# Output products with features on the partitions, in three passes of split operands, the first half's one behind Q and K of the next round

## What is computed

```python
xn  = layernorm(x)                                   # (4, 1024, 128)
q, k, v = heads(xn @ Wq), heads(xn @ Wk), heads(xn @ Wv)   # 16 heads of 64
w = softmax(causal(q @ k.T / 64))                    # per head
w = w * mask; w = w / (sum(w) + 1e-8)                # mask: a ramp over the keys
attn = merge_heads(w @ v) @ Wo                       # (4, 1024, 128)
ffn  = dequant(clip(round(xn / scale))) @ (ternary - 1).T + bias
out  = x + attn + ffn
```

## Time and profile before

| | |
|---|---|
| time, median of 3 runs | 1000.46 us (1000.36 to 1007.18) |
| the profiled execution's own time | 1000.45 us |
| its span in the trace | 998.7 us |
| PE busy | 983.3 us, 98% |
| DVE busy | 756.3 us, 76% |
| POOL busy | 706.4 us, 71% |
| ACT busy | 451.4 us, 45% |
| largest groups of the chain that ended last | G 25%, S 23%, M 12%, Y 7%, D 6% |

### The profile page before, as it was taken

The page is one execution under the profiler, slowest core; times in us unless marked ns, Lnnn a source line. Parts: engine busy times, 40 slices in busy tenths (PEclk is TensorE's granted clock), DMA queues, the critical chain, the costliest instruction groups (busy, mean ns, idle before and its releaser), DMA issues.

```text
span 998.7 us, 19217 instructions
## 1 busy us (share of the span) xinstructions
PE 983.3 (98%) x7125; PEld 633.6 (63%) x7125; DVE 756.3 (76%) x1706; ACT 451.4 (45%) x607; POOL 706.4 (71%) x649
## 2 busy tenths in 40 slices
PE   8999999999999999999999999999999999999997
PEld 4565666666666666666666666666666666666654
DVE  7877888878788878787767777777777667777754
ACT  4444445444444444454443454443454444454442
POOL 8766767767767667867766767667767667777672
PEclk9999999999999999999999999999999999999999
DMA  6000000000000000000000000000000000000000
GB/s 177 3 2 2 2 1 3 2 3 2 2 22 3 2 2 2 1 2 2 2 12 13 1 3 2 2 2 3 1 2 23 3 2 2 1 3 2 2 2 22
DMA packets 16133, 8.52 MB, mean 9 GB/s; under 512 B 5404, under 2 KB 15644, under 8 KB 16040
## 3 DMA queue, kind: packets, MB, share of 16 engines
q1 hardware_dynamic: 15416, 7.15, 2.6%
q10 hardware_dynamic: 624, 0.14, 0.1%
HBM read 4.33 MB, written 2.10 MB: 6 GB/s over the span
## 4 chain that ended last, share of the span: by engine, by line
PE 86%; DVE 9%; issue 2%; POOL 1%; ACT 1%; DMA 1%; DVEq 0%; SPq 0%; ACTq 0%; POOLq 0%
PE pv L1025 25%; PE ring L1008 23%; PE ring L970 12%; PE beside L1067 7%; PE beside L1040 6%; DVE ring L770 3%; PE ring L943 3%; PE ring L939 3%; PE ring L940 3%; DVE v L757 3%; DVE beside L794 1%; PE beside L1055 1%; PE beside L977 1%; PE ring L957 1%; PE ring L958 0%
## 5 line engine op out<-in xcount | busy, mean ns | idle before, releaser
L569 ACT ACTIVATE prob<-ring 128x1024 f32<-128x1024 f32 (+3 forms) x384 | 293.6, 810 | 346.7 <-PE ring L1008 346.6
L503 POOL TENSOR_TENSOR psumd<-psumd,prob 128x512 f32<-128x512 f32 (+1 forms) x250 | 406.2, 1625 | 28.9 <-POOL psumd L503 1.3
L770 DVE CUSTOM_DVE_ANT_0 ring<-ring,causal 128x128 f32<-128x128 f32 (+3 forms) x512 | 240.4, 517 | 97.1 <-PE ring L970 96.3
L1008 PE MATMUL ring<-q,k 64*128 64x512 f32 (+3 forms) x2304 | 279.8, 347 | 2.3 <-DMA mrow<-maxrow 0.8
L1025 PE MATMUL pv<-prob,v 128*64 128x512 f32 (+3 forms) x1536 | 267.1, 490 | 0.0
L476 POOL TENSOR_SCALAR_AFFINE_SELECT prob<-prob 128x256 f32<-128x256 f32 x256 | 109.4, 429 | 217.0 <-ACT prob L569 214.9
L1008 PEld LDWEIGHTS ring<-q,k 64*128 64x128 f32 x2304 | 194.6, 185 | 37.6 <-DVE rowmax L770 5.2
L1025 PEld LDWEIGHTS pv<-prob,v 128*64 128x64 f32 x1536 | 104.9, 137 | 154.1 <-issue 142.0
L774 DVE TENSOR_REDUCE rowmax<-ring 128x2 f32<-128x1024 f32 x128 | 151.4, 1222 | 3.9 <-PE ring L970 0.5
L499 POOL TENSOR_TENSOR psumd<-prob 128x768 f32<-128x768 f32 (+1 forms) x63 | 132.5, 2103 | 24.2 <-ACT prob L569 19.1
L970 PE MATMUL ring<-k,q 64*128 64x512 f32 (+3 forms) x768 | 142.9, 408 | 3.0 <-DVE k L746 0.7
(11 more groups left out here) (120 smaller groups left out, 943.3 us busy)
## 6 DMA issues: line engine op xcount, KB each, us to landing
kext<-kext SPq DMA_DIRECT2D x128, 4.0 KB, 1.7
out<-x_sb SPq DMA_DIRECT2D x8, 256.0 KB, 2.4
x_sb<-in_L_attn_query SPq DMA_DIRECT2D x3, 512.0 KB, 5.5
mrow<-maxrow SPq DMA_DIRECT2D x62, 4.0 KB
x_sb<-in_L_attn_query SPq DMA_DIRECT2D x2, 256.0 KB, 4.3
xn_sb<-in_L_attn_Wv SPq DMA_DIRECT2D x1, 512.0 KB, 5.2
wo<-in_L_attn_Wo SPq DMA_DIRECT2D x1, 512.0 KB, 7.0
xn_sb<-in_L_attn_Wq SPq DMA_DIRECT2D x1, 448.0 KB, 3.5
```

What stands on the lines that cost most here:

```text
L503: g.tensor_tensor(acc[:, :, lo:HALF], acc[:, :, lo:HALF], pr[:, :, lo:HALF], ALU.add).then_inc(acc_done, 1)
L569: a.activation(prob[n % NPROB][:, :, lo:HALF], ring[:, slot(f"S{t}", i), :, lo:HALF], ACT.Exp, scale=1.0 / DH).then_inc(exp_done, 1)
L770: last = v.tensor_tensor_reduce(out=ring[:, s, h, 0:n], in0=ring[:, s, h, 0:n], in1=causal[:, HALF - n:HALF], scale=1.0, scalar=MASKED, op ...
L1008: last = t_.matmul(ring[:, s, h, lo:HALF], k[p][rows, keys], q[p][rows, cols], start=(at == 0), stop=(at == len(parts) - 1))
```

## The change

Y of all pairs but the last one is now computed with features on the partitions: the weights `Wo` stand still, and the 512 tokens of a half move through in one matmul. Wo and the values are split as for Q and K, so that three float32r matmuls of 512 columns take the place of four float32 ones of 128. The products of a batch's pairs are summed in `yt` (in the place of xn of batch 0); after the last pair **P0** and **P1** turn the sum back on PE (4 transposes each), and DVE adds it to `x_sb`. The high part of the values (**h0**, **h1**) is a copy on ACT, the rest (**l0**, **l1**) a subtraction on DVE of two operands in SBUF. There is one buffer each for `o_sb`, its high part and its rest. The last pair keeps the old form.

The order changes too. Y0 goes from behind M9 to the next round, behind Q and K. Y1 goes from between M5 and M6 to where Y0 was. The quantisation runs one pair later, norm3 of the last batch moves to rounds 16 and 17, and Wo is loaded early, split on ACT and POOL in round 0 (**wo**). P stands in rounds 9, 17, 25 and 31.

```diff
-PE_PLAN = ("T Q+ K+ X0 X1 W G11- M0+ M1+ S0 S1 S2 M2+ D1- M3+ S3 V+ S4 S5 M4+ S6 M5+ Y1- M6+ M7+ S7 D0 G3 "
-           "M8+ S8 S9 S10 M9+ Y0 M10+ M11+ S11 G7")
-ACT_PLAN = "Z Qhi+ Khi+ X0 X1 E0 E1 E2 ln1- ex1- E3 E4 E5 E6 E7 ln0 ex0 E8 E9 E10 E11"
-DVE_PLAN = ("Tc Z Qlo+ Klo+ R0+ R1+ X0 X1 W R2+ R3+ t1- u1- Vs+ o1- R4+ R5+ Ya1- R6+ R7+ t0 u0 R8+ o0 q "
-            "R9+ R10+ Ya0 R11+")
-POOL_PLAN = "L0 A0 L1 A1 L2 A2 L3 A3 B0 A4 A5 A6 A7 L8 L9 L10 L11 A8 A9 A10 A11 B"
+PE_PLAN = ("T Q+ K+ P0 Y0- G11- P1 X0 X1 W M0+ M1+ S0 S1 S2 M2+ D1- M3+ S3 V+ S4 S5 M4+ S6 M5+ M6+ M7+ S7 D0 G3 "
+           "M8+ S8 S9 S10 M9+ Y1- M10+ M11+ S11 G7")
+ACT_PLAN = "Z Qhi+ Khi+ X0 X1 wo E0 E1 E2 ln1- ex1- E3 E4 E5 E6 h1- E7 ln0 ex0 E8 E9 E10 E11 h0"
+DVE_PLAN = ("Tc Z Qlo+ P0 Ya0- Klo+ P1 R0+ R1+ X0 X1 W R2+ R3+ t1- u1- Vs+ o1- R4+ R5+ R6+ R7+ l1- t0 u0 "
+            "R8+ o0 q R9+ R10+ Ya1- R11+ l0")
+POOL_PLAN = "L0 A0 L1 A1 L2 A2 L3 A3 B0 A4 A5 A6 A7 L8 L9 L10 L11 A8 A9 A10 A11 B wo"
...
-PE_LAST = "T G11- S0 S1 S2 D1- S3 S4 S5 S6 Y1- S7 D0 G3 S8 S9 S10 S11 Y0 D1 F1 G7 G11 Y1"
+PE_LAST = "T G11- S0 S1 S2 Y0- D1- S3 S4 P0 S5 S6 Y1- S7 D0 G3 S8 S9 P1 S10 S11 Y0 D1 F1 G7 G11 Y1"
-DVE_LAST = "Tc t1- u1- o1- A5 Ya1- A6 A7 t0 u0 o0 A8 A9 Ya0 t1 u1 o1 Ya1"
+DVE_LAST = "Tc q Ya0- t1- u1- o1- P0 A5 l1- A6 Ya1- A7 t0 u0 o0 P1 A8 A9 Ya0 t1 u1 o1 Ya1"
+ACT_LAST = "E0 E1 E2 ln1- ex1- E3 E4 h1- E5 E6 E7 ln0 ex0 E8 E9 E10 E11"
...
+            def values_high(i, c):
+                act.wait_ge(o_done, halves_upto(i, c))
+                if halves_upto(i, c) > 1:
+                    act.wait_ge(y_ready, halves_upto(i, c) - 1)
+                a.activation(o_hi[:, :], o_sb[:, :], ACT.Copy).then_inc(o_hi_done, 1)
...
+            def values_low(i, c):
+                dve.wait_ge(o_hi_done, halves_upto(i, c))
+                v.tensor_tensor(o_lo[:, :], o_sb[:, :], o_hi[:, :].bitcast(F32), ALU.subtract
+                                ).then_inc(o_lo_done, 1)
...
+                elif name == "wo":
+                    pool.wait_ge(wo_hi_done, 1)
+                    g.tensor_tensor(wo2[:, :, :].rearrange("p n d -> p (n d)"), yt,
+                                    wo1[:, :, :].rearrange("p n d -> p (n d)").bitcast(F32), ALU.subtract
+                                    ).then_inc(wo_lo_done, 1)
...
+            def turn_back(i, c):
+                b = batch_turned_back(i)
+                pe.wait_ge(y_added, halves_upto(min(b * NPB + NPB - 1, LAST - 1), c))
+                for k in range(HB):
+                    n = c * HB + k
+                    last = t_.transpose(beside[:, k * P:(k + 1) * P], yt[:, n * P:(n + 1) * P], ident[:, :])
+                last.then_inc(turned_back, 1)
...
             def output_projection(i, c):
...
+                if i < LAST:
+                    if i == 0 and c == 0:
+                        pe.wait_ge(wo_lo_done, 1)
+                    pe.wait_ge(o_hi_done, halves_upto(i, c))
+                    w_hi, w_lo = wo1[:, i % NPB, :], wo2[:, i % NPB, :]
+                    t_.matmul(beside[:, :], w_hi, o_hi[:, :], start=not with_ffn, stop=False)
+                    t_.matmul(beside[:, :], w_lo, o_hi[:, :], start=False, stop=False)
+                    pe.wait_ge(o_lo_done, halves_upto(i, c))
+                    last = t_.matmul(beside[:, :], w_hi, o_lo[:, :], start=False, stop=True)
```

More of the change, by code:

```diff
@@ L82, in happens @@
     if name == "q":
-        return i % PAIRS_OF_BATCH < PAIRS_OF_BATCH - 1
+        return i % PAIRS_OF_BATCH > 0
+    if name in ("P0", "P1"):
+        return i == LAST or i % PAIRS_OF_BATCH == 1 and i > PAIRS_OF_BATCH
+    if name == "wo":
+        return i == 0
+    if name == "wl":
+        return i == 2
+    if name in ("h0", "h1", "l0", "l1"):
+        return i < LAST
     if name == "Z":
@@ L97, in walk @@
     seen = set()
-    for i in range(-1, N_PAIRS + 1):
+    for i in range(-1, N_PAIRS + 2):
         for word in (first if i < 0 else plan if last is None or i < LAST else last).split():
@@ L111 @@
 IN_RING = [("X", -2)] + [u for u in PE_ORDER if u[0][0] in "QKSMV" or u == ("D1", LAST)]
-IN_BESIDE = [u for u in PE_ORDER if u[0][0] in "THDYXWF" and u not in (("D1", LAST), ("Y1", LAST))]
+IN_BESIDE = [u for u in PE_ORDER if u[0][0] in "THDYXWFP" and u not in (("D1", LAST), ("Y1", LAST))]
 PLACE = {u: n for n, u in enumerate(IN_RING)}
@@ L382, in _ @@
                     place_key_weights(i, i % 2)
+                elif name == "wl":
+                    sp.wait_ge(tern_done, 1)
+                    sp.dma_start(wo_last, wo_dram[(NPB - 1) * P:NPB * P, :]).then_inc(wo_last_landed, 16)
                 else:
                     b = i // NPB
[L385 to L388 removed]
+                    for c in range(2):
+                        if i == LAST:
+                            sp.wait_ge(y_added, halves_upto(i, c))
+                        else:
+                            sp.wait_ge(rows_added, 2 * b + c + 1)
+                        store(b, c * HB, (c + 1) * HB)
             sp.wait_ge(out_stored, 16 * 2 * B)
@@ L922, in turn @@
                 for k in range(HB):
-                    n = b * KB + c * HB + k
-                    last = t_.transpose(out[:, k * P:(k + 1) * P], xn_sb[:, n * P:(n + 1) * P], ident[:, :])
+                    n = c * HB + k
+                    last = t_.transpose(out[:, k * P:(k + 1) * P], xn_rows(b, n), ident[:, :])
                 last.then_inc(turned_ready, 1)
@@ L1053, in feed_forward @@
                 pe.wait_ge(fq_step, (i // NPB + 1) * FQ_STEPS)
+                if i < LAST:
+                    t_.matmul(beside[:, :], ternT[:, :], fq[:, c * HALF:(c + 1) * HALF], start=True, stop=False)
+                    return
                 for k in range(HB):
@@ L1060, in output_projection @@
                 with_ffn = i % NPB == NPB - 1
-                if i == 0 and c == 0:
-                    pe.wait_ge(wo_landed, 16)
                 if with_ffn and (f"F{c}", i) not in PLACE_BESIDE:
                     feed_forward(i, c)
-                pe.wait_ge(o_done, halves_upto(i, c))
-                for k in range(HB):
-                    last = t_.matmul(beside[:, k * P:(k + 1) * P], o_sb[c][:, k * P:(k + 1) * P],
-                                     wo[:, i % NPB, :], start=not with_ffn, stop=(not with_ffn or k == HB - 1))
+                if i < LAST:
+                    if i == 0 and c == 0:
[6 more added lines that the diff above has]
+                    last = t_.matmul(beside[:, :], w_hi, o_lo[:, :], start=False, stop=True)
+                else:
+                    pe.wait_ge(wo_last_landed, 16)
+                    pe.wait_ge(o_done, halves_upto(i, c))
+                    for k in range(HB):
+                        last = t_.matmul(beside[:, k * P:(k + 1) * P], o_sb[:, k * P:(k + 1) * P],
+                                         wo_last, start=not with_ffn, stop=(not with_ffn or k == HB - 1))
                 last.then_inc(y_ready, 1)
```

96 lines of the change are left out of this document (70 added, 26 removed).

## The result

| | before | after |
|---|---|---|
| time, median | 1000.5 us | 1035.14 us (1034.54 to 1037.09, 4 runs) |
| after : before, 95% interval | | 1.0342 [1.0318, 1.0367] |
| the profiled execution: time, span | 1000.45, 998.7 us | 1034.54, 1032.8 us |
| instructions on PE | 7125 | 6811 |
| one regular round, from T to T | 29.75 us | 30.18 us |

The ratio with its interval is taken over the single executions, not from the two medians. The change costs 3.4%. The forecast said 1025.0 us: the direction and the range held, and the size was 10 us too small.

What follows compares the result with a forecast made beforehand. PE, 98% busy, was taken as the bound, with DVE only some 0.2 us behind from M5 to S7. Terms 7.2 + 2.5 - 0.4 + 3.4 + 7.2 - 0.6 + 5.3 = 24.6 on 1000.4 gave 1025.0 us, range 1006 to 1040.

Steps and rivals of the forecast that it cites:

- Behind K: Regular round, Y0 placed behind Q and K: PE had no wait there, so its +0.70 us counts in full.
- Between M5 and M6: Regular round, Y1 leaves: of 1.09 us only 0.16 is saved, the rest becomes waiting for E6 and R5.
- The rival that Y1's place gives its time back: M7 and S7 don't wait, a regular round gains 0.69 us, total 997 us; chance 0.17.
- Behind M9: Regular round: Y0's 1.09 us there becomes Y1's 0.79, -0.30 a round.
- The shared port: DVE's l1 waits for POOL and makes t0 late: 0.3 us in 8 rounds, +2.5.
- The rival that l waits in every round: l loses 1.0 us to POOL each time, costing 17 instead of 2.5, total 1039 us; chance 0.13.
- Round 0: Round 0 loses Y0, but M10 and S11 come up against E9 and R9: -0.4 us.
- Round 1: The first Y0, and everything queued behind it on PE, waits for POOL's split of Wo: +3.4 us.
- the lower clock behind the wait: Rival: clock falls to 1.2 GHz in round 1's wait; Y0 and G11's 3.0 us doubles, 1028 us; chance 0.05.
- Rounds 9, 17, 25: Y0 waits for P0's bank and P1 adds 0.5: 2.3 us each, 0.3 more in round 17, +7.2.
- Last round: D1 waits for Y0 and Ya0, P0 for the bank, Y1's third pass for l1, delaying D0: +5.3 us.
- the feed-forward term: Six products with the feed-forward have fewer switches, -0.1 us each from the 1.09: -0.6.

Runs made afterwards that it cites:

- quarter of Y1: The kernel before with three of Y1's four matmuls left out in all pairs but the last: 997.73 us, ratio 0.9962.
- the move back: The changed kernel with Y0 moved from behind K to between M5 and M6, and its addition Ya0 behind R5: 1005.76 us, ratio 1.0059.
- order alone: The kernel before, with its old float32 Y, in the new order and with the quantisation one pair later: 1026.61 us, ratio 1.0248.
- the idle matmuls of round 1: The changed kernel with four unused float32 matmuls of 512 columns in PE's wait of round 1: 1032.89 us, ratio 1.0314.
- l on 8 columns: The changed kernel with l cut to 8 of 512 columns in all but the first half: 1038.26 us; same cut with Y0 between M5 and M6: 1001.93 us.
- Wo split early: The changed kernel with POOL's split of Wo moved from behind B to behind B0: 1031.07 us, ratio 1.0311.

## Why the prediction was right or wrong

**Behind K: right.** +0.71 for +0.70, three starts 0.23 apart and the switch. The addition Ya0 hid.

**Between M5 and M6: right, and the heart of it.** 1.09 us of work went, 0.16 of time. The released time turned into the wait that the forecast named, with R4 beside R5 and E6 as a releaser. The quarter of Y1 shows the same in the old kernel (0.06 a round for 0.8 of work), and the move back shows the other side (0.69 a round). The order alone, with the old instructions, has the same 1.83 from M5 to S7. The rival that Y1's place gives its time back (997 us) is refuted.

**S7 to D0: missed.** +0.13 where I had nothing. Before, PE came into S7 from M7 without a break; now S7 follows a wait, and its row of six stands with 0.96 busy where the earlier trace rows has 0.84. The rows show the same tenth elsewhere: the first matmul of 512 columns takes 0.50 instead of 0.39 and its successor starts 0.34 behind it, not 0.23, where it follows a wait or matmuls of another form (M7 in the earlier trace rows, Y1 behind M9 in the fence above, Y0 behind the idle matmuls of round 1). Before, the hole between M5 and M6 held no wait. Over 30 rounds this is 4 us. Two kernels with the old instructions show it too, the order alone (1.13) and the quarter of Y1 (1.12), so it comes with the wait and not with the new form. What inside PE takes it was not tried.

**Behind M9: mis-sized.** -0.19 for -0.30. Y1 there takes 957.07 - 956.17 = 0.90, not 0.79: three steps of 0.23, the switch on leaving, 0.09, and the same tenth on entry. The price was taken from K's last start, where passes alike precede and there is no entry to pay. Over 30 rounds it is 3 us. These two terms are the difference between +0.24 and +0.47.

**The shared port: the mechanism is there, the cost isn't.** l took 1.38 us in the mean, twice its shortest 0.68. The +2.5 were for the eight rounds with a heavy q, which are 5, 7, 13, 15, 21, 23, 29 and 31 of the changed kernel; with l on 8 columns the first seven are the same within 0.03. About 1.4 was real, but in rounds 2, 3, 9, 10 and the last: the size was near by luck, the place was wrong. The rival that l waits in every round was right on the wait and wrong on its price: 1039 needed t0's delay to reach S11, and DVE's slack took it up. The slack is where PE is slower: once Y0 had left the place behind K, rounds 8, 16 and 24 paid 0.5 to 0.8 us for the same l (by l on 8 columns).

**Round 0: right**, -0.3 for -0.4.

**Round 1: half of it missed.** +7.3 for +3.4 (and the 0.24 of each round). Y0 came 3.67 late, for 3.4. What was not in the sum is the lower clock behind the wait: 2.5 us. I had it as a rival, on top of the sum, with a price of 3.0 and a chance of 0.05, since the old trace had no idle stretch near this length; the price was about right, and the chance was the error. The last half a microsecond is there with Wo split early too (30.81) and was not resolved.

**Rounds 9, 17, 25: right in form, too small.** +10.3, of which 3 times 0.43 is the regular loss, so 9.0 for 7.2. In round 25 P0 starts at 811.23 and Y0 at 812.99, 1.76 us, where 1.75 was forecast. In round 9 it is more. PE's timelines of rounds 9 and 25, then DVE's of round 9:

```profile
314.98 0.60 PE L1147 MATMUL beside<-ident,xn_sb 128*128 128x128 f32 x4
317.55 0.50 PE L1171 MATMUL beside<-o_hi,wo 128*128 128x512 f32 x1 [1.97 <-DVE x_sb L880]
...
811.23 0.60 PE L1147 MATMUL beside<-ident,xn_sb 128*128 128x128 f32 x4
812.99 0.50 PE L1171 MATMUL beside<-o_hi,wo 128*128 128x512 f32 x1 [1.17 <-DVE x_sb L880]
```

```profile
312.75 3.03 DVE L731 TENSOR_SCALAR xn_sb<-x_sb,mv,rstd 128x128 f32<-128x128 f32 x4
315.69 1.21 DVE L808 TENSOR_TENSOR q<-ring,q 128x1024 fp32r<-128x1024 f32 x1
316.83 0.67 DVE L880 TENSOR_TENSOR x_sb<-x_sb,beside 128x512 f32<-128x512 f32 x1
```

The norm step of round 9 stands in DVE's queue ahead of Qlo, so the addition that frees the bank starts at 316.83, 1.85 behind P0's start. I had counted a norm step for round 17 alone, with 0.3. It stands in 9 too, before and after, and with it round 9 lost 3.5 and round 17 3.8 where round 25 lost 3.0: 0.6 and 0.9 for 0.3 in one. The four norm instructions took 3.03 us here, 758 ns each where the earlier trace rows has a median of 336. The kernel before shows most of that price, in its own round 9 (DVE's timeline):

```profile
302.37 2.78 DVE L669 TENSOR_SCALAR xn_sb<-x_sb,mv,rstd 128x128 f32<-128x128 f32 x4
```

**Last round: right in place, a little too large.** +4.55 for +5.3. D1 waits for the addition behind Y0, P0 for the bank, Y1's third pass for l1, as told. PE's timeline (D1, P0, third pass of Y1, D0), and DVE's A5:

```profile
999.42 1.08 PE L1131 MATMUL beside<-psumd,ones 128*64 128x512 f32 x4 [0.78 <-DVE xn_sb L893]
...
1003.32 0.66 PE L1147 MATMUL beside<-ident,xn_sb 128*128 128x128 f32 x4 [1.25 <-DVE rden L861]
...
1008.08 0.50 PE L1174 MATMUL beside<-o_lo,wo 128*128 128x512 f32 x1 [1.41 <-DVE o_lo L874]
...
1009.82 1.08 PE L1131 MATMUL beside<-psumd,ones 128*64 128x512 f32 x4
```

```profile
1006.20 1.23 DVE L926 TENSOR_TENSOR psumd<-prob 128x1024 f32<-128x1024 f32 x1 [1.50 <-ACT prob L618]
```

A5 took 1.23 where I used 1.96 of the earlier trace rows: coming later, it no longer met POOL's additions, the last of which ended at 1004.32. That is where most of the missing 0.7 lies. Counted from T, my steps had D1 at 7.5, A5 at 14.0, the third pass of Y1 at 16.7 and D0 at 18.8; they stood at 7.6, 14.4, 16.2 and 18.0. (The steps add up to 5.2 at D0, not to the 5.3 of the sum.)

**The sum.** Forecast +24.6, found +34.1: the 26 other rounds +12.4 (their share of my sum, with the port and the feed-forward term, about +8.1), round 1 +3.6 over its term, P +2.4 over its term and three regular rounds, and the last round 0.7 under. The feed-forward term of -0.6 can only be bounded: rounds 7, 8, 15, 16, 23 and 24 together grew by 2.3 us where six regular ones would grow by 2.6, with other units moved in them too. "22 us in all" for the instructions is 21.4 by the prediction's own terms, which changes nothing in its sum.
